# An audio-tower layer on one core: all attention products on VectorE, a reordered front, two more blocks of split weights

## What is computed

```python
h = einsum('bnp,dp->bnd', patches, W_tok) + b_tok            # 640 tokens x 512
x = layernorm(h);  q, k, v = x @ Wq.T, x @ Wk.T, x @ Wv.T    # q, k rotated
scores = q @ k.T / sqrt(32), causal (j <= i)
heavy  = the key with the largest sum of softmax(scores) over the queries
scores = where(heavy | (abs(i - j) <= 1), scores, min)       # the causal part stays
h = h + (softmax(scores) @ v) @ Wo.T
gate, up = split(layernorm(h) @ w_gate_up.T)
out = h + (silu(gate) * up) @ w_down.T
```

## Time and profile before

| | |
|---|---|
| median of 3 runs | 270.91 us (270.7 to 271.45) |
| the profiled execution's own time | 271.35 us |
| its span in the trace | 269.6 us |
| PE busy | 260.6 us, 97% of the span |
| PEld, DVE, ACT, POOL busy | 215.8, 168.7, 103.5, 51.6 us |
| granted TensorE clock | 1.00 |
| 57 to 70 us from the start | PE busy 12.37 of 13.00, DVE 11.72 |
| 91 to 152 us | PE busy 60.90 of 61.00, DVE 49.85, POOL 10.32 |

### The profile page before, as it was taken

The page is one execution under the profiler, slowest core; times in us unless marked ns, Lnnn a source line. Parts: engine busy times, 40 slices in busy tenths (PEclk is TensorE's granted clock), DMA queues, the critical chain, the costliest instruction groups (busy, mean ns, idle before and its releaser), DMA issues.

```text
span 269.6 us, 4974 instructions
## 1 busy us (share of the span) xinstructions
PE 260.6 (97%) x1893; PEld 215.8 (80%) x1893; DVE 168.7 (63%) x329; ACT 103.5 (38%) x174; POOL 51.6 (19%) x46
## 2 busy tenths in 40 slices
PE   7999999999889999999999999999999999999993
PEld 6565478885777877778788888999999999999992
DVE  0576998998879977779985864633333333333323
ACT  2311121561075445477731052643334433334320
POOL 0014000002055432100100001322333222222210
PEclk9999999999999999999999999999999999999999
DMA  6994130000038999986692041594333333400004
GB/s 195 418 414 161 69 118 1 5 2 0 0 99 179 303 269 267 287 241 219 188 232 101 1 146 50 145 337 143 117 118 117 117 117 118 123 32 0 0 0 117
DMA packets 12578, 37.51 MB, mean 139 GB/s; under 512 B 1616, under 2 KB 1616, under 8 KB 11920
## 3 DMA queue, kind: packets, MB, share of 16 engines
q1 hardware_dynamic: 11120, 32.15, 35.0%
q0 software_dynamic: 1152, 4.72, 9.4%
q10 hardware_dynamic: 288, 0.39, 0.4%
HBM read 31.23 MB, written 1.31 MB: 121 GB/s over the span
## 4 chain that ended last, share of the span: by engine, by line
PE 79%; DVE 14%; issue 3%; ACT 2%; POOL 1%; DVEq 0%; POOLq 0%
PE ps L221 50%; PE ps L1297 8%; PE ps L1278 5%; PE ps L1192 3%; PE ps L1100 3%; PE ps L1051 2%; DVE prod L249 2%; DVE stats L670 2%; PE ps L1212 1%; PE ps L1153 1%; PE ps L1122 1%; PE ps L1132 1%; PE ps L1106 1%; DVE xT L701 1%; POOL rs L364 1%
## 5 line engine op out<-in xcount | busy, mean ns | idle before, releaser
L221 PE MATMUL ps<-xT,wgu 128*128 128x384 f32 x384 | 70.5, 339 | 0.1
L221 PEld LDWEIGHTS ps<-xT,wgu 128*128 128x128 f32 x384 | 68.1, 188 | 1.8 <-issue 0.5
L914 DVE TENSOR_TENSOR gu<-silu,ps 128x256 f32<-128x256 f32 (+1 forms) x32 | 15.5, 485 | 50.5 <-PE ps L221 44.4
L358 POOL TENSOR_TENSOR wd<-stage,wd 128x512 fp32r<-128x512 f32 x16 | 26.2, 1637 | 77.1 <-ACT wd L430 77.1
L221 PE MATMUL ps<-wd,hT 128*128 128x512 f32 x156 | 38.8, 393 | 0.0
L569 ACT ACTIVATE silu<-ps 128x256 f32<-128x256 f32 (+1 forms) x32 | 14.1, 440 | 54.9 <-PE ps L221 50.4
L221 PEld LDWEIGHTS ps<-wd,hT 128*128 128x128 f32 x156 | 29.0, 188 | 5.4
L430 ACT ACTIVATE wgu<-stage 128x1024 fp32r<-128x1024 f32 x20 | 21.1, 1055 | 23.1 <-PE ps L221 23.1
L221 PE MATMUL ps<-xs,wgu 128*128 128x256 f32 x216 | 28.7, 289 | 0.1
L221 PEld LDWEIGHTS ps<-xs,wgu 128*128 128x128 f32 x216 | 26.1, 188 | 3.4 <-issue 1.9
L1297 PE MATMUL ps<-stage,gu 128*128 128x512 f32 x56 | 26.3, 592 | 0.0
(11 more groups left out here) (122 smaller groups left out, 325.9 us busy)
## 6 DMA issues: line engine op xcount, KB each, us to landing
stage<-w_ffn SPq DMA_DIRECT2D x32, 512.0 KB, 4.4
stage<-w_ffn SPq DMA_DIRECT2D x32, 256.0 KB, 3.6
wgu<-stage POOLq DMA_DIRECT2D x5, 512.0 KB, 6.4
stage<-w_k SPq DMA_DIRECT2D x1, 1024.0 KB, 6.9
stage<-w_q SPq DMA_DIRECT2D x1, 1024.0 KB, 10.3
stage<-w_v SPq DMA_DIRECT2D x1, 1024.0 KB, 12.4
wo<-w_o SPq DMA_DIRECT2D x1, 1024.0 KB, 13.9
wd<-stage POOLq DMA_DIRECT2D x2, 512.0 KB, 7.3
```

Of the source, the lines that this page charges most:

```text
L221: ins = pe.matmul(dst, lhs[a], rhs[b], start=first and n == 0, stop=last and n == 2)
L358: pool.tensor_tensor(dst, src, f32(hi), ALU.subtract).then_inc(done, 1)
L914: dve.tensor_tensor(gu[:, ring, cols], silu[:, ring, cols], ps[:, up, at:at + P * TILES[p]], ALU.mult)\
```

## The change

In parts:

- No product is made on POOL: `POOL_SCORES` and `POOL_VALUES` are gone; DVE makes group 1's products 5 and 7 in `scores`, and group 0's values 9 and 8 after block 1 of the first pass.
- `S1` goes from 4 to 2: blocks 2 and 3 of the first pass use split weights too. Their `minus_weights` stand on ACT ahead of `hi_attn(0)` and behind `hi_attn(1)`; their low parts' DMAs stand between POOL's powers.
- `hi_whole` and `low_whole` stand earlier; the drains of v of group 1 are spread over the first blocks.
- The minimum with the causal table is gone: a row of ones in `sums` (set once by a memset on DVE) times a row of 0 and -2^127 in `place` puts the causal part in through PE, and ACT copies the placed scores to `sm`.
- Query 9's sum is two reductions of five keys; the masked softmax of group 0 goes by queries 4 to 9 and 0 to 3 in place of 0 to 7 and 8, 9, with values 7 to 4 between the two.
- PE's order of folds, projections and biases is another; group 1's biases (and v's) come from a tile `spread` of 8 rows a part, which nine small DMAs on POOL's queue fill from `fold_bias`, times a constant `pick`.

```diff
-ROTATE = [item for item in PROJECT if item[0] != "v" and item[1] == 0]
+ROTATE = [("k", 0, 0), ("k", 0, 1), ("q", 0, 0), ("q", 0, 1), ("k", 0, 2), ("q", 0, 2)]
-POOL_SCORES = [(1, 5), (1, 7)]
-POOL_VALUES = [(0, 9), (0, 8)]
-SOFTMAX = [(0, 0, (0, 7)), (0, 0, (7, 10)), (0, 1, (0, 8)), (0, 1, (8, 10)),
+SOFTMAX = [(0, 0, (0, 7)), (0, 0, (7, 10)), (0, 1, (4, 10)), (0, 1, (0, 4)),
-S1, S2 = 4, 11
+S1, S2 = 2, 11
...
+            def spread_bias(x):
+                pool.wait_ge(fold_bias_set, x + 1)
+                for n in range(len(PARTS)):
+                    pool.dma_start(spread[GB * n:GB * n + 2 * NQ, x], fold_bias[0:P:GB // 2, x]).then_inc(dma_spread[x], 16)
...
             key_add(1)
+            spread_bias(0)
             key_add(2)
+            spread_bias(1)
+            spread_bias(2)
             power(3)
             power(4)
+            low_weights(2)
             power(LN2[1])
+            low_weights(3)
             power(LN2[0])
-            pool.wait_ge(turned, 2)
-            values(0, 9)
-            values(0, 8)
...
+            def place(n):
+                a, b = CHUNKS[n]
+                act.wait_ge(place_mm, n + 1)
+                if n == 0:
+                    act.wait_ge(sums_set, 2)
+                act.activation(sm[:, a:b].rearrange("p i h j -> p (i h j)"), ps[:, SCORE_BANK[n], 0:HQ * NPOS * (b - a)], ACT.Copy)\
+                   .then_inc(placed, 1)
...
             def minus_weights(i):
                 act.wait_ge(dma_stage[i % SLOTS], stage_count(A, i, i % SLOTS))
-                if i >= S1 + 3:
+                if i == S1:
+                    act.wait_ge(dma_spread[2], 16 * len(PARTS))
+                elif i == S1 + 1:
+                    act.wait_ge(tokens_mm, 1)
+                elif i == S1 + 2:
+                    act.wait_ge(project_mm, len(PROJECT))
+                elif i > S1 + 2:
                     act.wait_ge(gu_mm[A], 2 * (i - 2))
-                act.activation(gate_up_parts(i)[:, 1], stage[:, i % SLOTS, 0:2 * KT * P], ACT.Copy, scale=-1.0)
-                act.activation(gate_up_parts(i)[:, 0], stage[:, i % SLOTS, 0:2 * KT * P], ACT.Copy).then_inc(minus_set, 1)
+                act.activation(gate_up_parts(i)[:, 1], stage[:, i % SLOTS, 0:2 * KT * P], ACT.Copy, scale=-1.0)\
+                   .then_inc(minus_set, 1)
+                act.activation(gate_up_parts(i)[:, 0], stage[:, i % SLOTS, 0:2 * KT * P], ACT.Copy).then_inc(high_set, 1)
...
             softmax_out(2)
-            values(0, 7, 6, 5, 4, 3, 2, 1, 0)
+            values(0, 7, 6, 5, 4)
             softmax_out(3)
+            values(0, 3, 2, 1, 0)
...
             first_pass(0)
+            low_whole()
             first_pass(1)
             turn("k", 1)
+            values(0, 9, 8)
             scores(1, 0)
...
+            def project_biases(x, g):
+                m = "kqv".index(x)
+                pe.wait_ge(pick_set, 1)
+                pe.wait_ge(dma_spread[m], 16 * len(PARTS))
+                for n, (a, b) in enumerate(PARTS):
+                    rows = slice(GB * n, GB * n + 2 * NQ)
+                    dst = ps[:, PROJECT_BANK[PROJECT.index((x, g, n))], 0:DH * (b - a)].rearrange("p (i n) -> p i n", n=DH)
+                    pe.matmul(dst, pick[rows, :], repeated(spread[rows, m], 1, b - a), start=False, stop=True).then_inc(project_mm, 1)
...
-            value_sums(0, ("projection", ("q", 1, 0)))
-            value_sums(1, ("projection", ("v", 0, 2)))
-            project_out(1, 1, ("projection", ("k", 1, 1)))
+            value_sums(0, ("projection", ("k", 1, 2)))
+            project_tokens(("v", 1, 0), ("fold bias", 2))
+            project_out(1, 1, ("projection", ("k", 1, 0)))
+            value_sums(1, ("projection", ("q", 1, 0)))
+            project_tokens(("v", 1, 2), ("projection", ("k", 1, 1))).then_inc(tokens_mm, 1)
             project_out(0, 2, ("projection", ("q", 1, 2)))
```

More of the change, by code:

```diff
@@ L253, in value_number @@
         def value_number(item):
-            return sum((k in POOL_VALUES) == (item in POOL_VALUES) for k in VALUES[:VALUES.index(item) + 1])
+            return VALUES.index(item) + 1
         def stage_count(p, i, slot):
@@ L596, in _ @@
             first_pass(0)
-            hi_whole()
+            drain(("v", 1, 1))
             first_pass(1)
+            drain(("v", 1, 2))
             minus_weights(4)
@@ L859, in _ @@
             token_scale(2)
-            dve.memset(sm[:, :, :, :], -BIG)
+            dve.memset(sums[:, :, :], 1.0).then_inc(sums_set, 1)
+            dve.memset(sm[:, :, :, :], -BIG).then_inc(sums_set, 1)
             tables(0)
@@ L874, in _ @@
             early_products(9)
[L875 to L882 removed]
+            dve.wait_ge(product_set, NPOS)
+            step(last_scores(0, 5))
+            softmax_in(0)
+            step(last_scores(5, NPOS))
+            softmax_out(0)
+            softmax_in(1)
+            bias_join(2)
             softmax_out(1)
@@ L1121, in project_tokens @@
                     for q in range(NQ):
-                        pe.matmul(ps[GB * q:GB * (q + 1), bank, DH * (i - a):DH * (i - a + 1)], pat[:, col:col + GB],
-                                  fold[:, x, DH * q:DH * (q + 1)], start=i == a, stop=False)
+                        ins = pe.matmul(ps[GB * q:GB * (q + 1), bank, DH * (i - a):DH * (i - a + 1)], pat[:, col:col + GB],
+                                        fold[:, x, DH * q:DH * (q + 1)], start=i == a, stop=False)
+                return ins
             def project_bias(item):
@@ L1162, in score_place @@
                 pe.wait_ge(chunk_sb, n + 1)
-                pe.matmul(ps[:, SCORE_BANK[n], 0:HQ * NPOS * (b - a)], sums[0:rows, n],
-                          cut["place"][0:rows, HQ * NPOS * a:HQ * NPOS * b], start=True, stop=True).then_inc(place_mm, 1)
+                pe.matmul(ps[:, SCORE_BANK[n], 0:HQ * NPOS * (b - a)], sums[0:rows + 1, n],
+                          cut["place"][0:rows + 1, HQ * NPOS * a:HQ * NPOS * b], start=True, stop=True).then_inc(place_mm, 1)
             def spread_scale(g):
@@ L1244, in _ @@
-            project_parts("k", 1, ("fold", 2),
-                          ("chunk", 1), ("scores", 0))
-            project_parts("q", 1, ("scores", 1),
-                          ("projection", ("v", 0, 0)), ("projection", ("v", 0, 1)))
-            project_parts("v", 1, ("fold bias", 2),
-                          ("projection", ("k", 1, 2)), ("projection", ("q", 1, 1)))
-            value_sums(0, ("projection", ("q", 1, 0)))
-            value_sums(1, ("projection", ("v", 0, 2)))
-            project_out(1, 1, ("projection", ("k", 1, 1)))
+            score_sums(0, ("projection", ("q", 0, 0)))
@@ new lines, in _ @@
+            fold_weight_bias(2, 0, 1)
+            score_place(0, ("projection", ("q", 0, 1)))
+            score_sums(1, ("projection", ("k", 0, 2)))
+            fold_weight_bias(2, 2, 3)
+            score_place(1, ("projection", ("q", 0, 2)))
+            project_tokens(("v", 0, 0), ("fold", 2))
+            project_tokens(("v", 0, 1), ("embedding", 3))
+            project_tokens(("v", 0, 2), ("embedding", 4))
+            project_tokens(("k", 1, 0), ("chunk", 0))
+            project_tokens(("k", 1, 1), ("chunk", 1))
@@ new lines, in _ @@
+            for n in range(len(PARTS)):
+                project_bias(("v", 0, n))
+            project_tokens(("k", 1, 2), ("scores", 0))
+            project_biases("k", 1)
+            project_tokens(("q", 1, 0), ("scores", 1))
+            project_tokens(("q", 1, 1), ("projection", ("v", 0, 0)))
+            project_tokens(("q", 1, 2), ("projection", ("v", 0, 1)))
+            project_biases("q", 1)
+            project_tokens(("v", 1, 1), ("projection", ("v", 0, 2)))
+            value_sums(0, ("projection", ("k", 1, 2)))
@@ L1334, in _ @@
             transposes(LN2[1], ("wo", 1))
-            read_out("projection", ("k", 1, 0))
+            read_out("projection", ("q", 1, 1))
             pe.wait_ge(apart_set, NT)
@@ L1424, in lay_out @@
             place[row, i, n, j] = 1
+        place[row + 1, a:b] = np.where(pos[None, :] <= pos[a:b, None], 0, -LOWEST)[:, None, :]
     tables["place"] = place.reshape(P, -1)
```

134 lines of the change are left out of this document (63 added, 71 removed).

## The result

| | before | after |
|---|---|---|
| median of 20 runs each | 271.10 us | 268.47 us |
| ratio, 95% interval | | 0.9908 [0.9894, 0.9923] |
| the profiled execution's own time | 271.35 us | 268.19 us |
| its span | 269.6 us | 266.4 us |

The ratio is that of the runs in the fast state; two of the 20 after were slow, at 271.5 and 272.0. By it the change takes 2.5 us (0.92%, between 0.77 and 1.06%), by the medians 2.6; 1.8 was forecast, and 268.47 lies in the range.

What follows compares the result with a forecast made beforehand. PE, with 79% of the chain, was taken to bound the kernel. -0.4 us from the front and -1.4 from two split-weight blocks, POOL's products 0, gave -1.8: 270.9 to 269.1 us, range 267.9 to 270.3.

Steps and rivals of the forecast that it cites:

- the front: All work before PE's second stretch of 3.84 us blocks: claimed to bring that stretch 0.4 us earlier, to 74.6.
- k's projection: PE's front: second part's tokens fill the wait for the joined bias, so the fold of w_q starts 1.5 us earlier.
- The scores: Score stage on PE and DVE: sums start at 34.2 instead of 35.86, the second softmax step 1.4 us earlier.
- Masks and values: DVE's split masked softmax and values: values start about 53.45 instead of 54.98, rows with the softmax end 1.2 us earlier.
- The wait that comes next: ACT's drains and `minus_weights(2)` hold `hi_attn(0)` to 58.6; PE's series then starts tile 1's transposes 0.6 us earlier.
- v's biases: Three bias matmuls behind tile 0's transposes: 0.85 us, in PE's 0.67 wait for ACT's copy; 0.2 paid.
- second rival: The front gives all that DVE gains: DVE's `xn` sets the time, -1.2 at the transposes, 268.3 to 268.6; chance 0.15.
- Two blocks of split weights: First pass, blocks 2 and 3: 2.74 us instead of 3.45 each on PE, -1.4 in all.
- POOL's products: Products moved from POOL to DVE: 3.5 us of stall goes, DVE's first pass grows by 1.3, effect 0.
- The slack at block 2's `gu`: First pass, tightest place: DVE starts this product at about 85.6, PE asks at 87.4; slack 1.4 us.
- The third rival: DVE is late in the first pass if its stretching is not POOL's doing: 270 to 271 us; chance 0.10.
- ACT or PE waits for the bias transfers: Nine small POOL DMAs land late, between 50 and 55.6; slower, for instance 272 with landing at 60; chance 0.06.

Runs made afterwards that it cites:

- interleave: The changed kernel with k's first two parts back in the order tokens, bias, tokens, bias: 269.11 us, ratio 0.9913 to the kernel before.
- s1_4: The changed kernel with blocks 2 and 3 back in plain float32 matmuls: 269.64 us, ratio 0.9947 to the kernel before.
- unit_first: The changed kernel with ACT's copy of the first value unit ahead of `minus_weights(2)`: 268.51 us, ratio 0.9901 to the kernel before.
- one_rows: The changed kernel with a projection's three bias matmuls all reading the first eight partitions of `spread`: 269.06 us, ratio 0.9915 to the kernel before.
- before_dve: The kernel before with only POOL's two value and two score products moved to DVE: 271.11 us beside 271.49, ratio 0.9987.
- pool_products: The changed kernel with the four value and score products put back on POOL: 269.78 us, ratio 0.9972 to the kernel before.
- s2_10: The changed kernel with block 10's low gate and up weights from a DVE subtraction instead of a DMA: 268.51 us, ratio 0.9916 to the kernel before.
- v12_late: The changed kernel with v's last tokens moved behind tile 1's transposes, block 3's pieces behind tile 1: 269.14 us, ratio 0.9919 to the kernel before.

## Why the prediction was right, and where not

The direction and the range held. The sum (-1.8 for -2.5) is short by 0.7, and that is two errors of opposite sign: the front was underrated by 1.2, the first pass overrated by 0.3 to 0.6. That they partly cancel is luck. Of the front's 1.6 only the order of k's projection was undone by itself (interleave, 0.8); s1_4 shows the front's sum (1.4 against before), and its other parts are read from the timelines.

- **k's projection, -1.5.** Measured -1.8. The mechanism is right: undoing it alone costs 0.83, of which 0.47 is the wait. The step that was mis-sized is "both tokens end at about 17.5, both biases at 18.4": it added single pieces, 2.0 and 0.86, where same matmuls in a row take 1.75 and 0.66.
- **The scores, -1.65 and -1.4.** Measured -2.4 and -2.2 (second softmax step). 0.3 of that is inherited; the rest has the same root, by the chain after. The third parts of k and q, side by side, take 1.01 for their tokens and 0.43 for their biases, where the forecast added 0.57 twice and 0.32 twice, and the fold of w_v takes 3.44 for the 3.63 of the earlier trace rows.
- **Masks and values, -1.2 at the end of the values.** Measured -2.0: the values begin 2.4 earlier and give 0.4 back in the split softmax, where 0.3 was forecast.
- **"The wait that comes next": ACT holds `hi_attn(0)` to 58.6, -0.6 at the transposes.** This step failed. Aligned, 58.6 is 47.65 and the copy started at 46.58, 1.1 earlier. 0.9 of that is inherited: the drains begin that much earlier and take their 3.9. But the hold itself is 0.3 (unit_first) where the forecast had 0.8, and PE's v tokens, 1.0, lie over it; the order of the two is worth nothing. What the forecast said of the series behind (projection, sums, copy, projection, then the transposes at once) is what the timeline shows, and it does eat part of the gain: -3.1 at the first projection is -1.5 at the transposes. Against DVE's `xn` the series loses 0.5, where the forecast had 0.7 (67.4 against 68.1). So the forecast named the right engine here, and had DVE's gain too small: 1.2 for 2.0.
- **v's biases, 0.85, of which 0.2 were paid.** They take 0.50, and one_rows shows why; at 0.84 they would have cost nothing either. With this the front is -1.6 for "-0.4". The second rival (the front gives what DVE gains, 268.3 to 268.6) came nearest to the measured 268.47 by its number. Its condition came only by half: the sums and ACT were quicker, but DVE's `xn`, ready 0.5 before PE asked, did not set the time. Its price of -1.2 at the transposes was still too small, and the blocks gave less than it assumed.
- **Two blocks of split weights, -1.4.** On PE exactly that up to 89.25. At the end -0.8 to -1.1, by s1_4 and by the aligned spans. The step that failed is "one transfer per 4.5 us as before": PE comes to wait for a sum (0.88 and 0.39 in the two profiles, 0.24 in s1_4, none before), and its issue and landing stand on DMA engines that were 90% busy and are 95% busy now. That the full engines are what costs the 0.3 to 0.6 is read from the chain and not shown by an experiment. The profile before had the warning, in the windows above and in the 7.3 of the earlier trace rows; the forecast read the number for when a sum lands and not for what the engines had left.
- **POOL's products, 0.** Right for the move alone, as before_dve shows, and the rule of the Trainium skill ("SBUF — State Buffer", Who interferes with whom) agrees with these rows: a DVE instruction with two SBUF inputs stood while POOL's product ran (1.22 to 3.33, 0.69 to 2.36), and POOL's product stood when DVE's had begun (3.19). Not right for the whole: once `low_whole` stands early, as a float32r block 2 wants it, products on POOL cost 1.5 (pool_products). The edit is worth 0 alone and 1.5 beside the others, so the parts do not add up. The sum had the right value only because it took the stall as gone.
- **The slack at block 2's `gu`, 1.4.** 1.5 by the timeline. The third rival did not come.
- **ACT or PE waits for the bias transfers.** Neither did. POOL after, and the landing of those DMAs:

```profile
43.84 1.61 POOL L383 DMA_DIRECT2D spread<-fold_bias  x3 [7.23 <-DVE fold_bias L730]
```

```profile
spread<-fold_bias POOLq DMA_DIRECT2D x9, 4.0 KB, 2.0
```

The last are issued by 45.45 and in place at about 47.5, and ACT asks at 54.87. The 2.0 agrees with the estimate by the Trainium skill's fit ("DMA: Bandwidth & Descriptors", Anatomy of one DMA).

What stays open: what sets the length of the DMA wait and how much of it reaches the median (the profiles of s2_10 and v12_late have none, and neither kernel gains anything that can be measured), and whether the first or the second of the two new blocks brings more.

## What to carry to other kernels

When a stage is to be brought forward or its work moved to a form that needs another transfer, look at the DMA share of the stage it feeds into. Here it was 0.90, and a PE gain of 1.4 came out as 0.8 to 1.1; v12_late, with 0.95 and no wait, says that such a share is a warning and not a price. Costing pieces singly overrates a run of equal instructions, so take the duration from a row with the run's own length. And a move that is worth nothing alone may be what another edit rests on: try it both in the old order and taken out of the new one.

## What the hardware showed that was not expected

- **Seams between kinds of matmul.** Going from tokens to a bias and back costs PE some 0.2 each time, which no single row shows: 64 records of token matmuls in one run take 1.75 in the chain, two runs of 32 take 2.02; two biases 0.66 together and 0.86 apart.
- **Three 8-row matmuls side by side.** 0.50 on partitions 32 apart, 0.84 on the same ones. The Trainium skill tells of matmuls running together in different row groups ("TensorE: Matmul & The Clock Gate", Part 3: Packing small matmuls); the two runs show it here for three matmuls of unequal width.
- **The landing of a 512 KB sum** goes from 4.5 and 4.8 (DMA engines nearly idle) to 9.1 for one and the same transfer size within one execution.
- **What does not collide.** POOL issuing a DMA leaves DVE's products alone: from 79.46 to 80.34 POOL issues a sum while DVE's value products of 1280 and 1152 elements begin at 79.54. By 0.28 for 128 elements and 0.82 for 640 an estimate for the two is 1.49 and 1.36, and together they take 2.75.
